# A message-passing layer on one core: a fourth copy of the sums, and a new order of TensorE's steps

## What is computed

```python
h = jnp.maximum(_layernorm(x, axis=-1), 0.0)
# per edge
m = jnp.concatenate([h[col], edge_attr], axis=1)     # 64 + 64
m = jax.nn.relu(m @ W1.T + b1)                       # 128
m = jax.nn.relu(m @ W2.T + b2)                       # 128
# per node
summed = jax.ops.segment_sum(m, row, num_segments=n)
cnt = jax.ops.segment_sum(ones, row, num_segments=n)
agg = summed / jnp.maximum(cnt, 1.0)[:, None]
z = jax.nn.relu(jnp.concatenate([h, agg, u], axis=1) @ Wa.T + ba)
out = x + z @ Wb.T + bb
```

## Time and profile before

| | us |
|---|---|
| median of 3 runs | 2417.41 |
| the profiled execution | 2404.49 |
| its span, first to last instruction | 2402.7 |
| PE busy | 1894.7 (79%) |
| POOL busy | 1764.7 (73%) |
| DVE busy | 1289.1 (54%) |
| ACT busy | 954.8 (40%) |

### The profile page before, as it was taken

The page is one execution under the profiler, slowest core; times in us unless marked ns, Lnnn a source line. Parts: engine busy times, 40 slices in busy tenths (PEclk is TensorE's granted clock), DMA queues, the critical chain, the costliest instruction groups (busy, mean ns, idle before and its releaser), DMA issues.

```text
span 2402.7 us, 44999 instructions
## 1 busy us (share of the span) xinstructions
PE 1894.7 (79%) x12635; PEld 1565.7 (65%) x12840; DVE 1289.1 (54%) x4867; ACT 954.8 (40%) x2147; POOL 1764.7 (73%) x1131
## 2 busy tenths in 40 slices
PE   3788888888888888888888888888888879754546
PEld 2566666767766676767676677767677767553544
DVE  8655545555555555646555555555555656423227
ACT  2355544444434443444443444444443434311112
POOL 8477887777787777778777778787777777774370
PEclk8899999999999999999999999999999999876788
DMA  7688888988888888988888888988888889764446
GB/s 286 151 159 164 160 147 176 179 184 166 178 156 175 170 174 170 179 162 167 173 183 170 169 167 166 182 170 170 172 177 167 176 176 179 145 101 96 88 65 191
DMA packets 392057, 395.44 MB, mean 165 GB/s; under 512 B 51262, under 2 KB 296158, under 8 KB 391302
## 3 DMA queue, kind: packets, MB, share of 16 engines
q1 hardware_dynamic: 235030, 319.95, 48.3%
q0 software_dynamic: 155664, 71.47, 33.2%
q10 hardware_dynamic: 1120, 1.11, 0.2%
HBM read 221.11 MB, written 171.21 MB: 163 GB/s over the span
## 4 chain that ended last, share of the span: by engine, by line
POOL 33%; DMA 31%; issue 16%; PE 13%; DVE 4%; SPq 1%; ACT 1%; POOLq 0%; DVEq 0%; ACTq 0%
POOL sums L732 28%; DMA sums<-regA,idx 20%; DMA sums<-vscat,vidx 9%; POOL sums L720 4%; PE bank L1144 4%; PE bank L1183 3%; PE bank L1168 2%; PE bank L1157 2%; PE bank L1133 2%; DMA src<-rows_src 1%; DMA regC<-slots 1%; ACT h L828 1%; DVE regC L906 1%; DVE regC L986 1%; DVE regC L912 0%
## 5 line engine op out<-in xcount | busy, mean ns | idle before, releaser
L732 POOL DMA_INDIRECT sums<-regA,idx x904 | 1430.5, 1582 | 494.9 <-issue 232.5
L1183 PEld LDWEIGHTS bank<-w,h 128*128 128x128 f32 x3224 | 442.0, 199 | 151.4 <-issue 138.4
L1133 PE MATMUL bank<-h,regC 128*128 128x130 f32 x2832 | 397.4, 284 | 128.8 <-ACT h L828 128.8
L1133 PEld LDWEIGHTS bank<-h,regC 128*128 128x128 f32 x2832 | 352.6, 195 | 151.6 <-ACT h L828 151.6
L1183 PE MATMUL bank<-w,h 128*128 128x128 f32 x3224 | 439.7, 281 | 14.0 <-issue 4.2
L1168 PE MATMUL bank<-regA,L 128*128 128x512 f32 x806 | 435.4, 624 | 2.0 <-DVE regA L955 2.0
L1157 PE MATMUL bank<-h,regC 128*128 128x129 f32 x1808 | 260.0, 288 | 165.8 <-ACT vscat L837 135.0
L1144 PE MATMUL bank<-regC 120*128 120x129 f32 (+1 forms) x2352 | 314.6, 290 | 92.7 <-DVE regB L943 92.7
L828 ACT ACTIVATE h<-bank 128x512 f32<-128x512 f32 x403 | 241.1, 598 | 330.2 <-PE bank L1183 328.3
L804 ACT ACTIVATE regC<-bank 128x260 f32<-128x260 f32 x708 | 272.7, 386 | 244.3 <-PE bank L1133 187.5
L1144 PEld LDWEIGHTS bank<-regC 120*128 120x128 f32 (+1 forms) x2352 | 294.4, 203 | 104.1 <-issue 102.6
(11 more groups left out here) (140 smaller groups left out, 1339.2 us busy)
## 6 DMA issues: line engine op xcount, KB each, us to landing
regC<-slots SPq DMA_DIRECT2D x245, 243.8 KB
regA<-in_ea SPq DMA_DIRECT2D x202, 256.0 KB
slots<-regC SPq DMA_DIRECT2D x177, 260.0 KB
slots<-regC SPq DMA_DIRECT2D x177, 203.1 KB
src<-rows_src SPq DMA_DIRECT2D x226, 128.0 KB
dstR<-rows_dst SPq DMA_DIRECT2D x403, 64.0 KB
sums<-regA,idx POOLq DMA_INDIRECT x904
L<-p_table SPq DMA_DIRECT2D x403, 32.0 KB
```

The costliest lines, as they stand in the source:

```text
L732: nc.gpsimd.indirect_dma_start(out=sums[k], out_offset=bass.IndirectOffsetOnAxis(ap=idx[:, n % RING, t:t + 1], axis=0), in_=scat[:, n % 4, ...
L1133: last = T.matmul(psSlot(t)[:, k, :], place, h2[:, g % 2, t, :], start=True, stop=True)
L1183: last = T.matmul(psL2(g % 2)[:, t * H:(t + 1) * H], h1[:, g % 2, t * TILE:(t + 1) * TILE], w2[:, :], start=False, stop=t == TPG - 1)
```

## The change

- `NSETS` goes from 3 to 4; `ZAFTER` gets the 5 zeroing transfers of the fourth copy, in steps 5 to 7. The final addition adds two pairs of copies in one instruction of double width, and then the two halves.
- All odd groups from 3 to 367 are sorted (`SKIP` goes, `LAST_SORTED` 380 to 368): 183 sorted, 220 plain, 880 + 183 scatters. `BLOCK` is 31 (five blocks of 31 and one of 28, six blocks as before).
- Units stand on even steps only, at a step's end, at most one in a step; those of the last block one in each of the steps 376 to 400. `mid_unit` and `end_unit` go.
- `psVsum` moves to bank 1 beside `psUnit`; its matmul moves to the end of the step, and `free_last` goes. In its place the overflow sum waits for the last unit's addition (`acc_ready`), and a unit waits for the copy of the last overflow sum (`vscat_ready`).
- PE and ACT begin each step with the first layer, ahead of the work on group `s - 2`.

```diff
-NSETS = 3
+NSETS = 4
-ZAFTER = (0, 1, 1, 1, 1)
+ZAFTER = (0, 1, 1, 1, 1, 1, 2, 2)
-LAST_SORTED = 380
-SKIP_FROM, SKIP = 72, 24
+LAST_SORTED = 368
-BLOCK = 30
+BLOCK = 31
-    return 2 < g < LAST_SORTED and g % 2 == 1 and not (g >= SKIP_FROM and g % SKIP == SKIP - 1)
+    return 2 < g < LAST_SORTED and g % 2 == 1
-    firsts = [block[-1] + VREAD + 1 for block in BLOCKS]
+    firsts = [block[-1] + VREAD + 2 for block in BLOCKS]
-            s = firsts[k] + (firsts[k + 1] - firsts[k]) * q // UNITS if k + 1 < len(BLOCKS) else firsts[k] + q // 2
+            s = firsts[k] + 2 * ((firsts[k + 1] - firsts[k]) * q // (2 * UNITS)) if k + 1 < len(BLOCKS) else firsts[k] + q
+def units_until(s):
+    return sum(len(u) for at, u in UNITS_AT.items() if at <= s)
-        psVsum = bank[:, 7, 2 * W:2 * W + C]
+        psVsum = bank[:, 1, PAIR * C:(PAIR + 1) * C]
...
-                for k, q in end_unit(s - 1) + mid_unit(s):
+                for k, q in UNITS_AT.get(s - 1, ()):
                     add_unit(k, q)
...
-                    link(VE.tensor_tensor(s1[:, 0:m * C], SA[:, s, 0, 0:m * C], SA[:, s, 1, 0:m * C], ALU.add))
-                    link(VE.tensor_tensor(s2[:, 0:m * C], s1[:, 0:m * C], SA[:, s, 2, 0:m * C], ALU.add))
+                    link(VE.tensor_tensor(s1[:, :, 0:m * C], SA[:, s, 0:2, 0:m * C], SA[:, s, 2:4, 0:m * C], ALU.add))
+                    link(VE.tensor_tensor(s2[:, 0:m * C], s1[:, 0, 0:m * C], s1[:, 1, 0:m * C], ALU.add))
...
+                if is_sorted(s - VSUM):
+                    n = BINNED_NO[s - VSUM]
+                    pe.wait_ge(vmask_ready, n + 1)
+                    wait(pe, vscat_ready, n)
+                    wait(pe, acc_ready, units_until(s - 1))
+                    T.matmul(psVsum, vS[:, n % 2, :] if not general else zeros[:, 0:P], V[:, n % 2, 0:C], start=True, stop=True).then_inc(vsum_done, 1)
+                for k, q in UNITS_AT.get(s, ()):
+                    wait(pe, vscat_ready, sum(1 for g in BINNED if g <= s - VSUM))
                     add_up(k, q, general)
```

More of the change, by code:

```diff
@@ L139 @@
 assert LO * NBIN == NKEPT >= N and P < SLOTS <= PW and NG + max(VSUM, VLAG) < STEPS and LAST_SORTED <= 2 * ODD
-assert NBIN == BA * BA and PACK * BA <= P and NS % (4 * PACK) == 0 and max(len(u) for u in UNITS_AT.values()) <= 2
+assert NBIN == BA * BA and PACK * BA <= P and NS % (4 * PACK) == 0 and max(len(u) for u in UNITS_AT.values()) == 1
 def build(nc, x, src_cols, dst_cols, src_rows, dst_rows, ea, u, w1t, b1, w2t, b2, wat, ba, wbt, bb, out):
@@ L221, in build @@
         s2 = take(KC)
-        s1 = take(KC)
+        s1 = take(2 * KC).rearrange("p (k c) -> p k c", k=2)
         agg = take(2 * GE).rearrange("p (s r f) -> p s r f", s=2, f=H)
@@ L799, in evac_slots @@
                 act.wait_ge(slot_done, TPG * n + t + 1)
-                if t == 3 and is_sorted(g + 2 - VSUM):
-                    act.wait_ge(vsum_done, BINNED_NO[g + 2 - VSUM] + 1)
                 if t == 0:
@@ L806, in _ @@
             for s in range(STEPS):
+                if s < NG:
+                    act.wait_ge(l1_done, s + 1)
+                    wait(act, l2_done, s - 1)
+                    nc.scalar.activation(h1[:, s % 2, :], psL1(s % 2), ACT.Relu).then_inc(h1_ready, 1)
                 g = s - 2
@@ L817, in _ @@
                     evac_slots(g, 1)
[L818 to L821, removed]
                 g = s - 1
@@ L1107, in free_row @@
                 wait(pe, vmask_ready, sum(1 for g in BINNED if g <= s - VBC - 1))
-            def free_last(s):
-                wait(pe, vscat_ready, sum(1 for g in BINNED if g <= s - VSUM - 1))
             def bin_tile(g, t, general):
@@ L1121, in bin_tile @@
                     free_sums(g - 1)
-                    free_last(g + 2)
                     if general:
@@ L1148, in step @@
             def step(s, general):
[L1149 to L1161, removed]
                 if s < NG:
@@ L1174, in step @@
                         last.then_inc(l1_done, 1)
-                for k, q in mid_unit(s):
-                    add_up(k, q, general)
+                g = s - 2
+                if is_plain(g):
+                    n = PLAIN_NO[g]
+                    pe.wait_ge(h2_ready, g + 1)
+                    pe.wait_ge(mask_ready, n + 1)
+                    free_sums(g - 1)
+                    for t in range(TPG):
+                        last = T.matmul(bank[:, 6 + t // 2, (t % 2) * C:(t % 2 + 1) * C], S[:, n % 4, t, :], h2[:, g % 2, t, 0:C], start=True, stop=True)
+                    last.then_inc(sum_done, 1)
+                if is_sorted(g):
+                    bin_tile(g, 0, general)
+                    bin_tile(g, 1, general)
                 g = s - 1
@@ L1187, in step @@
                     bin_tile(s - 2, 3, general)
[L1188 to L1194, removed]
                 if is_sorted(s - VBC):
@@ L1213, in step @@
                     T.matmul(psOver, prefix[:, :], over[:, n % 2, :], start=True, stop=True).then_inc(over_done, 1)
-                for k, q in end_unit(s):
+                if is_sorted(s - VSUM):
[6 more added lines that the diff above has]
+                    wait(pe, vscat_ready, sum(1 for g in BINNED if g <= s - VSUM))
                     add_up(k, q, general)
```

## The result

| | us | ratio to before |
|---|---|---|
| before, in the comparison | 2416.81 (2414.14 to 2422.64), 4 runs | |
| after | 4453.99 (4452.19 to 4461.62), 4 runs | 1.8429, 95% interval 1.8389 to 1.8469 |
| predicted | 2200 (2165 to 2265) | 0.91 |

The change makes the kernel 84% slower. The direction and the size that I gave were wrong, and so was the mechanism at one step: a transfer that I had taken as unchanged.

A forecast was written before the change was run, and what follows sets the result against it. POOL was taken as the bound, at 1.886 us a scatter (9.43 a pair) plus waits. -137 + 20 - 34 - 78 + 13.5 = -215 us against a 2402.7 span gave 2187, adjusted to 2200 us; range 2165 to 2265.

The forecast's parts named there:

- part 3: PE feeding POOL in the loop: 8.75 us of work a pair, under POOL's 9.43; reordering and SP's queue costed at 0.
- part 4: End of the loop: one unit a step, 5.6 to 6.5 us a step, under POOL's 7.54: -78 us.
- the falling clock: Slower rival: PE's granted clock falls to 0.70, a pair takes 12.5 us, +550 us, about 2750; chance 0.03.
- part 1: POOL's waits for scatter landings: the fourth copy removes at most 137.4 us, with 20 us left: -137 + 20.
- part 2: POOL's scatters: 1081 become 1063, 18 x 1.886 = -34 us.
- part 5: Costs at both ends: fourth scatter delayed to 97.5 to 98 us, +5; double-width first addition, +8.5; together +13.5 us.
- the 20 us of caution: Landing waits expected to remain with four copies where DMA queues are fullest: 20 us, bounds 0 and 137.
- My rival for pairs held above the floor: Loop: DMA or rings at 0.95 hold pairs at 9.8 us, above POOL's 9.43; +48, 2248 us; chance 0.18.
- The Trainium skill's fixed cost for a DMA from GpSimd: Scatters: about 2.0 us plus bytes, 2.2 us, so the fourth copy gains nothing; +117, about 2317 us; no-effect chance 0.05.

## Why the prediction was wrong, point by point

**The step that failed is in part 3:** "SP's queue carries the units' reads as before, on even steps", and with it the 5.1 us from issue to data in part 4. The change makes the block 31 groups, and the prediction gives that edit no cost. The reads have the same queue and 3% more bytes, so I took them as the same. Their outer counts go from 30 and 120 to 31 and 124. The largest number up to 16 that divides both falls from 15 to 1, and the read runs on one DMA engine: 12.9 us alone instead of 3.5, and two reads a unit, which hold 24.46 us of the chain in the stretch shown further down. Blocks of 31 alone do this to the kernel before (4289.88 us), and blocks of 30 undo it in the changed one (2250.14). No rival had it; the one on the other side, the falling clock, named a consequence. The granted clock did fall to 0.70, between the levels of 1.2 and 2.4 GHz, but PE was busy only 42% of the time there because it waited for DVE, and with blocks of 30 it is 0.99.

The other terms are read in the kernel with blocks of 30, whose span is 2249.4 against 2402.7. By the prediction's sum, with 9 scatters more, it would take about 2217 us; it took 2250:

| term of the sum | predicted | with blocks of 30 |
|---|---|---|
| landing waits (part 1) | -137 + 20 | -137 |
| fewer scatters (part 2; 9 there, not 18) | -34 (18 x 1.886) | -17 (9 x 1.886, worked out) |
| SP and PE feed POOL (part 3) | 0 | +57 to +60 (70.0 less 44 gaps of 0.30, and small waits there) |
| end of the loop (part 4) | -78 | -78 |
| the fourth zeroing (part 5) | +5 | +5.5 |
| the final addition (part 5) | +8.5 | +9.6 |

Together -137 - 17 + 60 - 78 + 5.5 + 9.6 = -157, where the spans differ by 153.

- **Part 1 was right**, and the 20 us of caution weren't needed: 206 us fell to 1.2 us, and to 6.5 with the fourth copy alone. That the 20 us hide a third of what part 3 missed is luck. The Trainium skill's fixed cost for a DMA from GpSimd ("DMA: Bandwidth & Descriptors", "Anatomy of one DMA"), by which the fourth copy gives nothing, is refuted for scatters under this load by the 127 us.
- **Part 2 was right:** between blocks of 30 and 32, 18 scatters gave 33 us by the medians and 42 by the ratios.
- **Part 3 was wrong a second time, in a smaller way.** The reordering is worth about nothing, as costed, and PE could feed POOL. But SP's program did not feed the loop at that pace: I summed PE's work in a pair and never SP's, 6.6 us of issues in 10 and two reads of a row number between them. It cost some 60 us, until two loads left the queue and the pairs went to 9.5 us. My rival for pairs held above the floor foresaw the pace (9.8 us, and 9.89 was measured), and its 2248 us meet the 2250 of a kernel with 9 scatters more. But its reason, DMA at 0.95, is wrong, so that is luck: at 0.96 the pairs run at the floor.
- **Part 4 was right.** One unit a step: the last block's steps take 7.70 us in the changed kernel itself, where 7.54 were said, and POOL waits for no ACT copy of plain sums near the end.
- **Part 5 was right.** The fourth scatter starts at 99.40 us with blocks of 30 and at 100.82 in the changed kernel, somewhat later than the 98 said, against 94.08. The first addition takes 1163 ns instead of 657 as the mean of 13:

```profile
L1023 DVE TENSOR_TENSOR regC<-regA 128x1032 f32<-128x1032 f32 (+1 forms) x13 | 15.1, 1163 | 64.4 <-DMA regA<-sums 64.3
```

- **The range** rested on the five parts that I had costed. A range over the costed edits says nothing about the one that has no cost beside it.

## What to carry to other kernels

When a change alters a size, write down every transfer whose outer counts follow from it, and the largest number up to 16 that divides both sides. The prime counts 29, 31 and 127 put a read on one engine here, and what stands behind such a read pays too. Cut or pad such a transfer, or choose 30 or 32 for 31. Then sum each in-order queue over a period, SyncE's issues and the reads between them as well as the computing engines: what fed the bound with slack at the old pace may not at the new one.

## What the hardware showed that I had not expected

- A read of 31 x 4 rows, 252 KB, takes 12.8 to 13.1 us with nothing beside it, and 32 x 4 rows 3.18 us. 124 rows flat take 5.0 us.
- An issue behind such a read is held up on SP itself: 8.60 us for a 32 KB load at 2020.95 and some 12 us in the longest pieces of the chain that ended last (start us, us), against some 0.5 us. The slow transfer costs its queue's issuing time as well as its own:

```profile
393.32 11.83 SPq L497
504.46 24.46 DMA regC<-slots
547.42 12.60 SPq L497
```

- Moving 200 loads of 256 KB and 220 of 128 KB from SP's queue to ACT's makes the kernel with four copies faster (2250 to 2190 us) and the one with three slower (2288 to 2357 us). Why is open.
